# A graph network on one core: the preparation moved into the first gathers, and hop 0 with single outer products

## The chip, the cores and the metric

The kernel runs on one core of one Trainium2 chip. The metric is the device time of one execution in microseconds. Before the change three runs took 1715.54, 1716.27 and 1716.9 us; the median is 1716.27 us.

## The reference, cut to what matters

There are 50,000 nodes with 64 features and 25,000 edges (src, dst), sorted by dst. Layer 0 sums the normalised rows of the sources over each destination and puts every node through a small two-layer network. Layer 1 is an attention over three hops, with 8 heads of 8 features. What the change touches is the preparation of the degrees and hop 0:

```python
deg = segment_sum(ones, col, n);  deg_inv = where(deg > 0, deg ** -0.5, 0)
norm = deg_inv[row] * deg_inv[col] * edge_weight
Kj = relu(K[row] + ef)
M = segment_sum(norm * einsum('ehi,ehj->ehij', Kj, V[row]), col, n)   # hop 0
K = segment_sum(norm * Kj, col, n)
# hops 1 and 2:  M = segment_sum(norm * M[row], col, n)
```

## The kernel before, in words

The edges lie in 196 tiles of 128, and four tiles (EH) make a unit, so that each sweep has 49 units. Each engine runs one loop over a common tick `g`. All stages hang on that tick, and the order of the work on an engine is the order in which its loop body is written; semaphores tie the engines together. There is no planner.

- Ticks 0 to 48: the source rows of the edges are gathered by GpSimd (L541), normalised and kept in SBUF. Beside it VectorE and ScalarE do one unit of dense nodes every two ticks, and ScalarE counts the slot of each source (the `Sign` calls at L688).
- Ticks 49 to about 108: the destination rows are gathered, summed over equal destinations by TensorE and put through the network. The new row of each edge goes to `node_rows` in HBM.
- Ticks 109 (C0) to 159: hop 0. GpSimd gathers `node_rows` by source (L555). TensorE turns the rows (L947, L950), and makes keys, values and queries (L931 to L939). ScalarE copies keys (L718) and scaled values (L721) from PSUM banks 6 and 7 (`pkz`) to a ring of three SBUF tiles (`kvz`). VectorE makes the outer products of keys and values into PSUM banks 0 to 3, two tiles at once (`outer`, L1146), and adds each to the running sum (`join`, L1154). SyncE stores 1 MB of state (L501) and 256 KB of keys and values (L497) a unit. The function called at `NORMS_AT` makes the edge norms of two units in three small operations (L1300, L1307, L1313).
- Then hop 1 (D0), hop 2 (E0) and the output: gather the state, scale it, multiply by the queries. In hop 1 VectorE alternates L1354 (add) and L1356 (multiply).

The preparation of degrees is on VectorE in tick 55 (`PREP`): `prep_slots` (L1035 to L1062) passes the work to and fro between VectorE and TensorE three times (L918 to L924). In tick 56 ScalarE takes a root (L699) and `prep_rows` a reciprocal. In ticks 58 to 85 SyncE writes degrees and destinations into `node_rows`, 28 DMAs of 7 KB in pieces of 8 bytes (L457). `prep_out` is in tick 105, `prep_tiles` in tick 9. TensorE's preparation used bank 6, which also holds the segment ends until tick 53.

Of the kernel before, what the change touches and what calls it, by code (L numbers as in the profile page):

```python
# [14 lines left out]
P = 128  # L15
N = 50000
E = 25000
D = 64
# [51 lines left out]
PREP = B0 + 6  # L70
TAIL_AT = {PREP + 3 + i: i * TAIL for i in range(T // TAIL)}
# [113 lines left out]
def gnn(nc, x, edge_w, edge_attr, src_tm, dst_tm, dst_tmf, dst_row, ends, ends_col, masks, dst_pm, src_pm, src_row,  # L185
# [4 lines left out]
    d_tab, d_x1, d_kv = dram("node_rows", (ROWS, TW)), dram("x1_rows", (ROWS, D)), dram("kv_rows", (P, CU * 2 * W))  # L190
# [9 lines left out]
    with ExitStack() as ctx:  # L200
# [57 lines left out]
        kvz = ring("kv", [P, 2, EH, D], 3, s_front)  # L258
# [37 lines left out]
        kvf, thf, xf, hTf = (ring("kv_back", [P, 2, EH, D], RB, s_out), ring("row_back", [P, EH, D], RB, s_out),  # L296
# [22 lines left out]
        pprep = bank[6]  # L319
# [61 lines left out]
        def _(sync):  # L381
# [27 lines left out]
            def load_back(u):  # L409

                c = slice(u * EH, (u + 1) * EH)
                wait(sync, scaled_f, u - RB + 1)
                wait(sync, chained, EH * (u - RB + 1) + 1)
                sync.dma_start(gg[u % RB][:, 1, :, :], by_slot(d_g[1])[:, c, :]).then_inc(back_in[u % RB], 16)
                wait(sync, g0_set, u - RB + 1)
                sync.dma_start(kvf[u % RB][:, :, :, :].rearrange("p c k f -> p (c k f)"), d_kv[:, u * 2 * W:(u + 1) * 2 * W]).then_inc(back_in[u % RB], 16)
# [28 lines left out]
            for g in range(END + 1):  # L445
# [49 lines left out]
                if 0 <= u < CU:  # L495
                    sync.wait_ge(v_done, u + 1)
                    sync.dma_start(d_kv[:, u * 2 * W:(u + 1) * 2 * W], kvz[u % 3][:, :, :, :].rearrange("p c k f -> p (c k f)")).then_inc(kv_kept[u % 3], 16)  # L497
# [110 lines left out]
        def _(act):  # L608
# [13 lines left out]
            for g in range(END + 1):  # L622
# [74 lines left out]
                if g == PREP + 1:  # L697
                    act.wait_ge(prep_v, 3)
                    act.activation(tmp2[:, :], tmp[:, :], ACT.Sqrt).then_inc(prep_a, 1)  # L699
# [12 lines left out]
                if 0 <= u < CU:  # L712
                    p = pkz[u % 2]
                    act.wait_ge(kv_z, u + 1)
                    wait(act, outered, EH * (u - 2))
                    wait(act, kv_kept[u % 3], landed(u - 3, u % 3, 3))
                    parts = p[:, :].rearrange("p (k c f) -> p k c f", c=2, f=D)
                    act.activation(kvz[u % 3][:, 0, :, :], parts[:, :, 0, :], ACT.Relu).then_inc(k_done, 1)  # L718
                    act.wait_ge(wn_set, NORMED[u])
                    for k in range(EH):  # L720
                        ins = act.activation(kvz[u % 3][:, 1, k, :], parts[:, k, 1, :], ACT.Copy,  # L721
                                             scale=wn0[:, u * EH + k:u * EH + k + 1])
                    ins.then_inc(v_done, 1)
# [71 lines left out]
        def _(ten):  # L795
# [20 lines left out]
            for g in range(END + 1):  # L816
# [87 lines left out]
                if m is not None:  # L904
                    ten.wait_ge(h1_d, m + 1)
                    if m == LATE:
                        ten.wait_ge(prep_v, 3)
                    wait(ten, copied2_d, m)
                    turn_dense(turn2_bank(m), h1d[m % 2], turned2_d)
# [5 lines left out]

                if g == PREP:
                    ten.wait_ge(fixes_out, 1)
                    ten.matmul(pprep[:, 0:P], dpm[:, 0:1].to_broadcast([P, P]), ident[:, :], start=True, stop=True)  # L918
                    ten.matmul(pprep[:, 3 * P:3 * P + 1], shift[:, :], dpm[:, 0:1], start=True, stop=True).then_inc(prep_pe, 1)
                    ten.wait_ge(prep_v, 1)  # L920
                    ten.transpose(pprep[:, P:2 * P], carry[:, :], ident[:, :])
                    ten.matmul(pprep[:, 3 * P + 1:3 * P + 2], carry[:, :], tmp[:, T - 1:T], start=True, stop=True).then_inc(prep_pe, 1)
                    ten.wait_ge(prep_v, 2)
# [3 lines left out]
                if 0 <= u < CU:  # L927
                    p = pkz[u % 2]
                    wait(ten, v_done, u - 1)
# [95 lines left out]
        def _(vec):  # L1025
# [7 lines left out]
            def prep_slots():  # L1033
# [18 lines left out]
                vec.tensor_tensor(tail[:, :, 0], tmp[:, :], islast[:, :], ALU.mult).then_inc(prep_v, 1)  # L1052
                vec.wait_ge(prep_v, 1)
# [3 lines left out]
                vec.tensor_copy(carryT[:, :], pprep[:, P:2 * P]).then_inc(prep_v, 1)  # L1057
                vec.wait_ge(prep_v, 2)
# [80 lines left out]
            def outer(u, k):  # L1139

                shape = [P, 2 * HEADS, HD, HD]
                keys = flat(kvz[u % 3][:, 0, k:k + 2, :]).rearrange("p (c i) -> p c i", i=HD).unsqueeze(3).to_broadcast(shape)
                values = flat(kvz[u % 3][:, 1, k:k + 2, :]).rearrange("p (c j) -> p c j", j=HD).unsqueeze(2).to_broadcast(shape)
# [17 lines left out]
            for g in range(END + 1):  # L1161
# [98 lines left out]
                if g == 9:  # L1260
                    prep_tiles()
                if g == PREP:
                    prep_slots()
                if g == PREP + 1:
                    prep_rows()
                if g == C0 - 4:
                    prep_out()
# [113 lines left out]
                if 0 <= u < CU:  # L1381
                    vec.wait_ge(back_in[u % RB], back_rows(u))
                    o = slice(u * EH, (u + 1) * EH)
                    own.add(vec.tensor_tensor(kq[:, :, :], kvf[u % RB][:, 0, :, :], Q[:, o, :], ALU.mult))
# [15 lines left out]
                if 0 <= u < CU:  # L1400
# [3 lines left out]
                                      kvf[u % RB][:, 1, :, :].rearrange("p t (h j) -> p t h j", j=HD),  # L1404
# [116 lines left out]
```

## Time and profile before

| what | us |
|---|---|
| median of three runs | 1716.27 |
| the profiled execution | 1718.93 |
| its span | 1716.3 |
| VectorE busy | 1447.0 (84%) |
| TensorE busy | 1305.7 (76%) |
| GpSimd busy | 1208.4 (70%) |
| ScalarE busy | 990.9 (58%) |

The profiled execution is 2.7 us over the median. An engine's share is a mean over stages that have different limits, so each stage has to be read by itself: the window table gives busy time for a stretch, and the timeline gives start and length of each instruction with the idle time before it.

### The profile page before, as it was taken

How to read it: one execution, taken by the hardware profiler on the slowest of the kernel's cores; microseconds unless marked ns; L12 is line 12 of the kernel's file. 1: busy time of each engine (PE TensorE's matmuls, PEld its weight loads, DVE VectorE, ACT ScalarE, POOL GpSimd, SP SyncE). 2: the span in 40 equal slices, each digit the busy share in tenths (PEclk: the TensorE clock that was granted, in tenths of full speed). 3: DMA queues.
4: the chain of work that ended last, by engine and by line, in shares of the span. 5: the costliest groups of instructions: out<-in, count | busy, mean ns of one | idle time of the engine just before them, and what ended most of it. 6: DMA issues, size and time to landing. Idle time of an engine off the chain costs nothing. (4 is left out here: it accounts for less than half of the span.)

```text
span 1716.3 us, 21669 instructions
## 1 busy us (share of the span) xinstructions
PE 1305.7 (76%) x5794; PEld 800.1 (47%) x5794; DVE 1447.0 (84%) x2713; ACT 990.9 (58%) x2643; POOL 1208.4 (70%) x1185
## 2 busy tenths in 40 slices
PE   3889888899888757877863777775787999777771
PEld 3666666666666534544541233332233444455541
DVE  5888888799999849999997999995557788799991
ACT  4998987599999724444442555553555566233330
POOL 7777777577774077777736777774777777777776
PEclk8999998899999868878785889898798999888886
DMA  5444444477775459999985888885344544466640
GB/s 131 112 123 124 125 124 108 109 164 160 161 171 144 106 149 304 305 296 304 292 285 175 287 309 306 303 299 204 94 143 143 154 140 145 138 176 172 179 134 16
DMA packets 281215, 313.80 MB, mean 183 GB/s; under 512 B 169009, under 2 KB 198569, under 8 KB 268550
## 3 DMA queue, kind: packets, MB, share of 16 engines
q1 hardware_dynamic: 224166, 246.39, 46.6%
q0 software_dynamic: 56928, 66.04, 15.0%
q8 instruction: 47, 0.77, 0.2%
q14 instruction: 74, 0.61, 0.1%
HBM read 214.54 MB, written 161.32 MB: 219 GB/s over the span
## 5 line engine op out<-in xcount | busy, mean ns | idle before, releaser
L973 PE MATMUL bank<-product,ident 128*128 128x512 f32 (+1 forms) x800 | 385.0, 639 | 136.7 <-DVE product L1356 136.7
L579 POOL DMA_INDIRECT state<-state_hop,slot_of_src x392 | 396.4, 1011 | 125.8 <-issue 107.8
L748 ACT ACTIVATE bank<-state,norm 128x512 f32<-128x512 f32 x392 | 251.1, 679 | 255.4 <-DMA state<-state_hop,slot_of_src 218.9
L1356 DVE TENSOR_TENSOR product<-bank,queries 128x512 f32<-128x512 f32 x392 | 261.0, 687 | 91.3 <-ACT bank L748 89.8
L973 PEld LDWEIGHTS bank<-product,ident 128*128 128x128 f32 x800 | 162.1, 207 | 357.1 <-issue 186.2
L555 POOL DMA_INDIRECT row_of_src<-node_rows,pos_int x196 | 214.5, 1094 | 118.6 <-DMA node_rows<-row_new 59.1
L541 POOL DMA_INDIRECT x_edges<-in_x,dst_tiles x196 | 198.0, 1010 | 84.5 <-issue 48.0
L541 POOL DMA_INDIRECT x_edges<-in_x,src_tiles x196 | 198.5, 1013 | 62.6 <-issue 59.4
L595 POOL DMA_INDIRECT out<-rows,dst_out x196 | 194.7, 993 | 59.8 <-issue 58.2
L1354 DVE SCALAR_TENSOR_TENSOR acc<-acc,same_as_before,bank 128x512 f32<-128x512 f32 x196 | 144.9, 740 | 15.7 <-ACT bank L748 15.0
L1154 DVE SCALAR_TENSOR_TENSOR acc<-acc,same_as_before,bank 128x512 f32<-128x512 f32 x196 | 146.5, 747 | 12.3
L1015 PE MATMUL bank<-gg_squares,ident 128*128 128x256 f32 x294 | 100.1, 490 | 55.8 <-DVE gg_squares L1430 55.8
L1146 DVE TENSOR_TENSOR bank<-kv 128x1024 f32<-128x1024 f32 x98 | 120.3, 1227 | 5.1 <-ACT kv L721 4.7
L808 PE MATMUL bank<-bias_three,ones_three 3*128 3x512 bf16 (+1 forms) x246 | 83.7, 340 | 38.2 <-DVE x_edges L1254 23.6
L873 PE MATMUL bank<-dst_steps,from_here 128*128 128x197 f32 x392 | 85.0, 364 | 22.3 <-DVE end_flags L1123 17.1
L1015 PEld LDWEIGHTS bank<-gg_squares,ident 128*128 128x128 f32 x294 | 66.2, 240 | 74.9 <-DVE gg_squares L1430 65.1
L718 ACT ACTIVATE kv<-bank 128x256 f32<-128x256 f32 x49 | 18.8, 384 | 124.6 <-PE bank L936 118.4
L808 PEld LDWEIGHTS bank<-bias_three,ones_three 3*128 3x128 bf16 x246 | 22.6, 92 | 130.4 <-issue 126.0
L1420 DVE SCALAR_TENSOR_TENSOR gg<-gg,same_as_before 128x192 f32<-128x192 f32 x196 | 81.2, 414 | 2.0
L774 ACT ACTIVATE gg_squares<-gg 128x768 f32<-128x768 f32 x49 | 41.2, 840 | 68.1 <-DVE gg L1420 68.1
L873 PEld LDWEIGHTS bank<-dst_steps,from_here 128*128 128x128 f32 x392 | 69.2, 203 | 24.0 <-issue 21.8
L688 ACT ACTIVATE bank<-bank,src_slots 128x196 f32<-128x196 f32 x196 | 75.8, 387 | 4.9 <-PE bank L873 4.6
(219 smaller groups left out, 2844.4 us busy)
## 6 DMA issues: line engine op xcount, KB each, us to landing
state_hop<-acc SPq DMA_DIRECT2D x98, 1024.0 KB, 4.6
x_nodes<-in_x SPq DMA_DIRECT2D x49, 256.0 KB, 4.1
src_row<-in_src_row SPq DMA_DIRECT2D x49, 256.0 KB, 3.6
out<-out_rows SPq DMA_DIRECT2D x49, 256.0 KB, 4.2
dst_row<-in_dst_row SPq DMA_DIRECT2D x49, 256.0 KB, 3.6
kv_rows<-kv SPq DMA_DIRECT2D x49, 256.0 KB, 3.3
gg<-head_sums SPq DMA_DIRECT2D x98, 128.0 KB, 2.9
kv_back<-kv_rows SPq DMA_DIRECT2D x49, 256.0 KB, 2.9
```

Of the source, the lines that this page charges most:

```text
L541: pool.indirect_dma_start(out=xe[b][:, 0, k, :], out_offset=None, in_=x, in_offset=bass.IndirectOffsetOnAxis(ap=index[:, t:t + 1], axis=0) ...
L555: pool.indirect_dma_start(out=tg[u % RT][:, k, :], out_offset=None, in_=d_tab[0:SLOTS, :], in_offset=bass.IndirectOffsetOnAxis(ap=posi[:, ...
L579: pool.indirect_dma_start(out=mg[u % 4][:, k, :], out_offset=None, in_=d_m[hop - 1], in_offset=bass.IndirectOffsetOnAxis(ap=sidx[:, t:t + ...
L595: pool.indirect_dma_start(out=out, out_offset=bass.IndirectOffsetOnAxis(ap=dst_out[:, t:t + 1], axis=0), in_=rowf[u % NR][:, k, :], in_off ...
L748: act.activation(pw[t % len(pw)][:, :], mg[u % 4][:, k, :], ACT.Copy, scale=wn12[:, t:t + 1]).then_inc(weighted, 1)
L873: ins = ten.matmul(pair[:, 256 * k:256 * k + T + 1], gsel[u % 2][:, k * P:(k + 1) * P], delta[:, :], start=True, stop=True, skip_group_che ...
L973: ins = ten.matmul(ph[:, 0:k * D].rearrange("p (c j) -> p c j", j=HD), ident[:, :], part, start=(r == 0), stop=(r == HD - 1))
L1015: ins = ten.matmul(p[:, 0:W], ident[:, :], sqf[u % 3][:, :, :].rearrange("p (k c) j -> p k (c j)", k=HOPS)[:, k, :], start=False, stop=(k ...
L1146: vec.tensor_tensor(to, keys, values, ALU.mult).then_inc(outered, 2)
L1154: vec.scalar_tensor_tensor(accz[u % 3][:, k, :], before, same[:, t:t + 1], prz[k][:, :], ALU.mult, ALU.add).then_inc(acc_z, 1)
L1354: vec.scalar_tensor_tensor(acch[u % 3][:, k, :], before, same[:, t:t + 1], pw[t % len(pw)][:, :], ALU.mult, ALU.add).then_inc(acc_h, 1)
L1356: vec.tensor_tensor(ihj(pr[m % 2][:, u % 2 * EH + k, :]), ihj(pw[t % len(pw)][:, :]), over_j(Q[:, t, :]), ALU.mult).then_inc(multiplied, 1)
```

## The change

The preparation is cut up: `prep_slots` becomes three functions, called at VectorE's ticks 4, 6 and 8; `prep_rows` goes to tick 10, `prep_out` to 24, `prep_tiles` from 9 to 30. TensorE's part goes to ticks 3, 5 and 7 and to bank 7, ScalarE's root to tick 9, and the 28 DMAs of L457 to ticks 12 to 39. In hop 0 one outer product covers one tile, reads its values from PSUM (where ScalarE now scales them in place) and its keys from SBUF. Outer products and accumulations alternate, and the last accumulation of a unit follows the first outer product of the next. TensorE may overwrite the bank of keys and values of unit u-2 only when the outer products of u-2 are done. ScalarE copies the scaled values to SBUF in one further operation, for the store. The stored keys and values have another order in HBM, with pieces of the same size.

```diff
-PREP = B0 + 6
-TAIL_AT = {PREP + 3 + i: i * TAIL for i in range(T // TAIL)}
+TAIL_AT = {12 + i: i * TAIL for i in range(T // TAIL)}
...
-        kvz = ring("kv", [P, 2, EH, D], 3, s_front)
+        kvz = ring("kv", [P, EH, 2 * D], 3, s_front)
...
-        pprep = bank[6]
+        pprep = bank[7]
...
-                if g == PREP + 1:
+                if g == 9:
                     act.wait_ge(prep_v, 3)
                     act.activation(tmp2[:, :], tmp[:, :], ACT.Sqrt).then_inc(prep_a, 1)
...
-                    act.activation(kvz[u % 3][:, 0, :, :], parts[:, :, 0, :], ACT.Relu).then_inc(k_done, 1)
+                    act.activation(kvz[u % 3][:, :, 0:D], parts[:, :, 0, :], ACT.Relu).then_inc(k_done, 1)
                     act.wait_ge(wn_set, NORMED[u])
                     for k in range(EH):
-                        ins = act.activation(kvz[u % 3][:, 1, k, :], parts[:, k, 1, :], ACT.Copy,
+                        ins = act.activation(parts[:, k, 1, :], parts[:, k, 1, :], ACT.Copy,
                                              scale=wn0[:, u * EH + k:u * EH + k + 1])
-                    ins.then_inc(v_done, 1)
+                    own.add(ins)
+                    own.sync()
+                    act.activation(kvz[u % 3][:, :, D:2 * D], parts[:, :, 1, :], ACT.Copy).then_inc(v_done, 1)
...
+                    if m == 0:
+                        ten.wait_ge(prep_v, 3)
                     if m == LATE:
-                        ten.wait_ge(prep_v, 3)
+                        ten.wait_ge(fixes_out, 1)
...
-                    wait(ten, v_done, u - 1)
+                    wait(ten, outered, EH * (u - 1))
...
             def outer(u, k):
-                shape = [P, 2 * HEADS, HD, HD]
-                keys = flat(kvz[u % 3][:, 0, k:k + 2, :])...to_broadcast(shape)
-                values = flat(kvz[u % 3][:, 1, k:k + 2, :])...to_broadcast(shape)
-                to = quad[:, MW * k:MW * (k + 2)].rearrange("p (c i j) -> p c i j", i=HD, j=HD)
-                wait(vec, acc_z, EH * (u - 1) + k + 2)
-                vec.tensor_tensor(to, keys, values, ALU.mult).then_inc(outered, 2)
+                vs = pkz[u % 2][:, (2 * k + 1) * D:(2 * k + 2) * D]
+                wait(vec, acc_z, EH * (u - 1) + k + 1)
+                vec.tensor_tensor(ihj(prz[k][:, :]), over_j(kvz[u % 3][:, k, 0:D]), over_i(vs), ALU.mult).then_inc(outered, 1)
...
                     outer(u, 0)
+                if 0 < u < CU:
+                    join(u - 1, 3)
...
                 if 0 <= u < CU:
+                    outer(u, 1)
                     wait(vec, m0_kept[u % 3], landed(u - 3, u % 3, 3))
                     join(u, 0)
...
                 if 0 <= u < CU:
+                    outer(u, 2)
                     join(u, 1)
-                    outer(u, 2)
+                    outer(u, 3)
                     join(u, 2)
+                if u == CU - 1:
                     join(u, 3)
```

## Rows read from the trace of the kernel before

**Rows 1.** Windows of 50 us: busy us (count) by engine, then clock, DMA share, GB/s.
```profile
core 0: us, PE busy (x) PEld busy (x) DVE busy (x) ACT busy (x) POOL busy (x), PEclk, DMA share, GB/s
150.00:200.00 50.00, 44.01 (x298) 33.68 (x297) 42.84 (x78) 46.41 (x163) 38.42 (x39) 1.00 0.45 122
...
450.00:500.00 50.00, 44.31 (x287) 30.12 (x287) 49.55 (x114) 46.90 (x125) 35.15 (x36) 1.00 0.76 170
...
700.00:750.00 50.00, 38.88 (x194) 24.83 (x196) 47.70 (x66) 23.85 (x94) 39.31 (x36) 0.83 0.96 304
...
800.00:850.00 50.00, 40.58 (x190) 25.61 (x189) 46.31 (x68) 22.37 (x86) 39.34 (x36) 0.76 0.92 297
```

**Rows 2.** Waits of 120 to 180 us: total us, times, longest.
```profile
DVE stats L1184 <- ACT stats L695: 8.7, 6, 2.6
```

**Rows 3.** VectorE's timeline, ticks 5 and 6: start, length, instruction, idle before it.
```profile
38.82 1.22 DVE L1227 TENSOR_REDUCE stats<-x_nodes 128x16 f32<-128x1024 f32 x1 [1.84 <-ACT x_nodes L703]
...
44.22 0.30 DVE L1184 RECIPROCAL stats<-stats 128x24 f32<-128x24 f32 x1 [1.97 <-ACT stats L695]
```

**Rows 4.** VectorE's timeline, ticks 55 and 56.
```profile
311.24 0.16 DVE L1036 COPY next_first<-bank 128x1 f32<-128x1 f32 x1 [4.82 <-PE bank L919]
...
318.06 0.30 DVE L1184 RECIPROCAL stats<-stats 128x24 f32<-128x24 f32 x1
...
323.27 1.37 DVE L1067 RECIPROCAL dinv_slots<-prep_tmp 128x196 f32<-128x196 f32 x1
...
325.02 1.21 DVE L1224 TENSOR_REDUCE stats<-x_nodes 128x16 f32<-128x1024 f32 x1
```

**Rows 5.** ScalarE's timeline: the root that VectorE needs, ticks 55 and 105.
```profile
309.80 0.31 ACT L695 ACTIVATE stats<-stats,eps_col 128x24 f32<-128x24 f32 x1
...
589.69 0.32 ACT L695 ACTIVATE stats<-stats,eps_col 128x32 f32<-128x32 f32 x1 [0.63 <-DVE stats L1241]
```

**Rows 6.** VectorE's timeline, tick 105: first of prep_out, first after it.
```profile
589.56 0.35 DVE L1073 TENSOR_REDUCE prep_cols<-in_first 128x1 f32<-128x196 f32 x1
...
593.62 0.35 DVE L1184 RECIPROCAL stats<-stats 128x32 f32<-128x32 f32 x1
```

**Rows 7.** VectorE's timeline in hop 0: unit 1, one pair of units, the end.
```profile
629.87 1.29 DVE L1146 TENSOR_TENSOR bank<-kv 128x1024 f32<-128x1024 f32 x1 [0.41 <-issue]
...
742.22 0.16 DVE L1300 TENSOR_TENSOR dinv_of_src<-row_of_src,src_slots 128x8 f32<-128x8 f32 x1
...
746.43 1.53 DVE L1154 SCALAR_TENSOR_TENSOR acc<-acc,same_as_before,bank 128x512 f32<-128x512 f32 x2
...
753.47 0.16 DVE L1300 TENSOR_TENSOR dinv_of_src<-row_of_src,src_slots 128x8 f32<-128x8 f32 x1
...
903.04 0.26 DVE L1322 TENSOR_SCALAR prep_tmp<-dinv_of_src 128x196 f32<-128x196 f32 x1
```

**Rows 8.** VectorE's timeline in hop 1, alternating order, two steps apart.
```profile
948.30 0.75 DVE L1354 SCALAR_TENSOR_TENSOR acc<-acc,same_as_before,bank 128x512 f32<-128x512 f32 x1
...
950.82 0.74 DVE L1354 SCALAR_TENSOR_TENSOR acc<-acc,same_as_before,bank 128x512 f32<-128x512 f32 x1
```

**Rows 9.** The page's groups: busy us, mean ns of one, idle before, releaser.
```profile
L579 POOL DMA_INDIRECT state<-state_hop,slot_of_src x392 | 396.4, 1011 | 125.8 <-issue 107.8
...
L555 POOL DMA_INDIRECT row_of_src<-node_rows,pos_int x196 | 214.5, 1094 | 118.6 <-DMA node_rows<-row_new 59.1
...
L718 ACT ACTIVATE kv<-bank 128x256 f32<-128x256 f32 x49 | 18.8, 384 | 124.6 <-PE bank L936 118.4
```

**Rows 10.** TensorE's timeline in hop 0: the first matmul of four units.
```profile
747.01 0.37 PE L931 MATMUL bank<-bias_three,ones_three 3*128 3x512 bf16 x1 [0.89 <-ACT rows_turned L733]
...
751.57 0.37 PE L931 MATMUL bank<-bias_three,ones_three 3*128 3x512 bf16 x1 [0.88 <-ACT rows_turned L733]
...
816.08 0.58 PE L931 MATMUL bank<-bias_three,ones_three 3*128 3x512 bf16 x1 [1.60 <-ACT rows_turned L733]
...
823.44 0.58 PE L931 MATMUL bank<-bias_three,ones_three 3*128 3x512 bf16 x1 [0.78 <-ACT rows_turned L733]
```

**Rows 11.** Waits of 630 to 900 us: total us, times, longest.
```profile
ACT kv L721 <- DVE norm L1313: 20.7, 12, 6.1
```

More of the change, by code:

```diff
@@ L188, in dram @@
         return nc.dram_tensor(name, shape, F32, kind="Internal").ap()
-    d_tab, d_x1, d_kv = dram("node_rows", (ROWS, TW)), dram("x1_rows", (ROWS, D)), dram("kv_rows", (P, CU * 2 * W))
+    d_tab, d_x1, d_kv = dram("node_rows", (ROWS, TW)), dram("x1_rows", (ROWS, D)), dram("kv_rows", (SLOTS, 2 * D))
     d_m = [dram("state_hop0", (SLOTS, MW)), dram("state_hop1", (SLOTS, MW))]
@@ L295, in gnn @@
         qf = ring("norms", [P, 4, NH], 3, s_out)
-        kvf, thf, xf, hTf = (ring("kv_back", [P, 2, EH, D], RB, s_out), ring("row_back", [P, EH, D], RB, s_out),
+        kvf, thf, xf, hTf = (ring("kv_back", [P, EH, 2 * D], RB, s_out), ring("row_back", [P, EH, D], RB, s_out),
                              ring("x1_back", [P, EH, D], RB, s_out), ring("back_turned", [P, W], 3, s_out))
@@ L415, in load_back @@
                 wait(sync, g0_set, u - RB + 1)
-                sync.dma_start(kvf[u % RB][:, :, :, :].rearrange("p c k f -> p (c k f)"), d_kv[:, u * 2 * W:(u + 1) * 2 * W]).then_inc(back_in[u % RB], 16)
+                sync.dma_start(kvf[u % RB][:, :, :], by_slot(d_kv)[:, c, :]).then_inc(back_in[u % RB], 16)
                 wait(sync, turned_f, u - RB + 1)
@@ L496, in _ @@
                     sync.wait_ge(v_done, u + 1)
-                    sync.dma_start(d_kv[:, u * 2 * W:(u + 1) * 2 * W], kvz[u % 3][:, :, :, :].rearrange("p c k f -> p (c k f)")).then_inc(kv_kept[u % 3], 16)
+                    sync.dma_start(by_slot(d_kv)[:, u * EH:(u + 1) * EH, :], kvz[u % 3][:, :, :]).then_inc(kv_kept[u % 3], 16)
                 u = g - C0 - 2
@@ L914, in _ @@
                     turn_dense(ptd, zd[m % 2], turned1_d)
-                if g == PREP:
-                    ten.wait_ge(fixes_out, 1)
+                if g == 3:
                     ten.matmul(pprep[:, 0:P], dpm[:, 0:1].to_broadcast([P, P]), ident[:, :], start=True, stop=True)
                     ten.matmul(pprep[:, 3 * P:3 * P + 1], shift[:, :], dpm[:, 0:1], start=True, stop=True).then_inc(prep_pe, 1)
+                if g == 5:
                     ten.wait_ge(prep_v, 1)
@@ L922, in _ @@
                     ten.matmul(pprep[:, 3 * P + 1:3 * P + 2], carry[:, :], tmp[:, T - 1:T], start=True, stop=True).then_inc(prep_pe, 1)
+                if g == 7:
                     ten.wait_ge(prep_v, 2)
@@ L1052, in prep_slots, with prep_ends @@
                 vec.tensor_tensor(tail[:, :, 0], tmp[:, :], islast[:, :], ALU.mult).then_inc(prep_v, 1)
+            def prep_ends():
                 vec.wait_ge(prep_v, 1)
@@ L1057, in prep_slots, with prep_degrees @@
                 vec.tensor_copy(carryT[:, :], pprep[:, P:2 * P]).then_inc(prep_v, 1)
+            def prep_degrees():
                 vec.wait_ge(prep_v, 2)
@@ L1139, in outer @@
             def outer(u, k):
-                shape = [P, 2 * HEADS, HD, HD]
-                keys = flat(kvz[u % 3][:, 0, k:k + 2, :]).rearrange("p (c i) -> p c i", i=HD).unsqueeze(3).to_broadcast(shape)
-                values = flat(kvz[u % 3][:, 1, k:k + 2, :]).rearrange("p (c j) -> p c j", j=HD).unsqueeze(2).to_broadcast(shape)
-                to = quad[:, MW * k:MW * (k + 2)].rearrange("p (c i j) -> p c i j", i=HD, j=HD)
-                wait(vec, acc_z, EH * (u - 1) + k + 2)
-                vec.tensor_tensor(to, keys, values, ALU.mult).then_inc(outered, 2)
+                vs = pkz[u % 2][:, (2 * k + 1) * D:(2 * k + 2) * D]
+                wait(vec, acc_z, EH * (u - 1) + k + 1)
+                vec.tensor_tensor(ihj(prz[k][:, :]), over_j(kvz[u % 3][:, k, 0:D]), over_i(vs), ALU.mult).then_inc(outered, 1)
             def join(u, k):
@@ L1259, in _ @@
                     prep_bias()
-                if g == 9:
-                    prep_tiles()
[L1262 to L1267, printed above, removed]
+                if g == 4:
+                    prep_slots()
+                if g == 6:
+                    prep_ends()
+                if g == 8:
+                    prep_degrees()
+                if g == 10:
+                    prep_rows()
+                if g == 24:
+                    prep_out()
+                if g == 30:
+                    prep_tiles()
                 if g == CU + 3:
@@ L1383, in _ @@
                     o = slice(u * EH, (u + 1) * EH)
-                    own.add(vec.tensor_tensor(kq[:, :, :], kvf[u % RB][:, 0, :, :], Q[:, o, :], ALU.mult))
+                    own.add(vec.tensor_tensor(kq[:, :, :], kvf[u % RB][:, :, 0:D], Q[:, o, :], ALU.mult))
                     n_kq = own.n
@@ L1403, in _ @@
                     vec.tensor_tensor(gg[u % RB][:, 0, :, :].rearrange("p t (h j) -> p t h j", j=HD),
-                                      kvf[u % RB][:, 1, :, :].rearrange("p t (h j) -> p t h j", j=HD),
+                                      kvf[u % RB][:, :, D:2 * D].rearrange("p t (h j) -> p t h j", j=HD),
                                       scf[:, :].rearrange("p (t h) -> p t h", h=HEADS).unsqueeze(3).to_broadcast(
```

## The prediction, made before the changed kernel was run

> **What bounds the kernel now.** I read the window table first, then the waits of the stretches that differ, then the timelines of the engines where the change works, and last the page's groups for prices.
>
> The table [rows 1] separates three regimes. In the first gathers (150 to 200 us) no engine is full: ScalarE has 46.4 of 50 us and VectorE 42.8. The waits [rows 2] show VectorE held up by ScalarE's root, 8.7 us in six times, 1.45 us each time, once in two ticks. So VectorE has about 1.4 us to spare in two ticks and the stage goes round in a VectorE-ScalarE loop. In the second gathers (450 to 500 us) VectorE is busy 49.55 of 50 us: whatever it does there is time. In hop 0 (700 to 750 us) VectorE has 47.7 of 50 us, the DMA engines a share of 0.96, and TensorE a clock of 0.83, which is a mix of its two levels, 2.4 and 1.2 GHz.
>
> **The preparation: what goes.** In tick 55 VectorE waits 4.82 us for TensorE and then goes to and fro with it until 318.06 [rows 4]. ScalarE's root for that tick was done at 309.80 + 0.31 = 310.11 [rows 5]; it is what is late next. So 318.06 - 310.11 = 7.9 us go, of which I take 7.5, since ScalarE has a remainder of its tick to finish. In tick 56 `prep_rows` stands from 323.27 to 325.02 on the full VectorE: 1.75 us. In tick 105 `prep_out` stands from 589.56 to 593.62, 4.06 us [rows 6], while the root it hides was done at 589.69 + 0.32 = 590.01 [rows 5]: 3.5 us go, in the drain that the gathers of hop 0 wait for. Sum 12.7 us.
>
> **The preparation: what comes.** The parts are called at the end of even ticks, ahead of the large reductions, so a part's length is paid less what VectorE would have waited for ScalarE.
> - Tick 4: `prep_slots` without its ends, some 3.9 us (L1036 at 311.24 [rows 4] to the first answer of TensorE). VectorE waits 1.84 and 1.97 us in the next tick and a half [rows 3]: 3.8 us of cover, 0.1 us left. TensorE's answer was given a tick earlier.
> - Ticks 6 and 8: about 1.0 us each, under 1.4 us of cover: 0.
> - Tick 10: `prep_rows`, 1.75 - 1.4 = 0.4 us. ScalarE's root in tick 9 is one 0.3 us operation on the engine with the least room: 0.3 us.
> - Tick 24: `prep_out`, 4.06 - 1.4 = 2.7 us.
> - Tick 30: `prep_tiles`, four operations, about 1.5 us: 0.1 us more; in tick 9 it was covered too.
> - The 28 small DMAs move from a stretch with a DMA share of 0.76 to one with 0.45 [rows 1]. They stand on SyncE behind loads that are two ticks ahead of their use: 0. If that cover failed, each load would come up to some tenths late, 28 times: 5 us at most.
>
> Sum 3.6 us; bounds 0 (all covered) and 12 (no cover). Loops like this one do not catch up later, so I keep it as permanent. Net of the preparation: -9 us, between -13 and -1.
>
> **Hop 0 on VectorE.** From unit 1 to the end is 903.04 - 629.87 = 273.2 us for 48 units, 5.69 a unit; a pair takes 753.47 - 742.22 = 11.25 us [rows 7]. Two accumulations in a row take 1.53 us [rows 7], the second waits for the first. The alternating order stands in hop 1: from one L1354 to the next but one is 2.52 us, so an accumulation and a product cost 1.26 us [rows 8], with nothing waited for. The product there has one operand in PSUM, as the new one, and writes to SBUF, where the new one writes to PSUM; no row has that form. Its cost a step lies between 1.26 us and the present mean of 11.25 / 8 = 1.41 us; I take 1.26, being the same engine and size. Four steps make 5.04, the norms (three small operations for two units, their waits now hidden under a neighbour) 0.15: 5.2 us a unit, where 5.62 stood.
>
> **Hop 0 elsewhere.** What is late next?
> - GpSimd. A gather takes 1.011 us in hop 1 and 1.094 us in hop 0 [rows 9]; with 0.3 us of issue (107.8 us over 392) that is 1.31 or 1.39 us, four to a unit: 5.2 or 5.6 us. GpSimd is as slow as VectorE now, not slower. If the longer ones are held up by the products with both operands in SBUF, they fall to 1.31; I take 5.25 us.
> - DMA. The share 0.96 of 5.65 us is 5.4 us of work a unit. A share near one also counts queueing, so the floor is between 5.0 (no limit) and 5.4.
> - The loop of TensorE and ScalarE. At the high clock a unit takes 751.57 - 747.01 = 4.56 us, at the low clock 823.44 - 816.08 = 7.36 us [rows 10]. ScalarE gets one more copy of 256 columns, 0.38 us [rows 9], and a wait for its own result, some 0.1 us: 5.0 and 7.8 us. Before, TensorE could be nearly two units ahead of VectorE; now it may start a unit only after the products of the last but one, so it has one VectorE unit, 5.2 + 0.7 us, for a chain that takes about 4 us at the high clock and 6 at the low. Units at the low clock were mostly hidden; now each costs 7.8 - 5.35 = 2.45 us.
>
> I take 5.35 us for a unit at the high clock, which is 257 us for 48. How many units are at the low clock decides the rest. Before, the clock was 0.83 over the five windows from 650 to 900 us (0.76 in the last of those shown [rows 1]): a third of the time, some 13 units. Those stretches began after TensorE had stood still for 1.6 us and more, as at 816.08 [rows 10]; with gaps of 0.9 us it stayed at the high level. The long gaps came where ScalarE ran into the norms, 20.7 us in 12 waits [rows 11]; with TensorE held nearer to VectorE they mostly go. The new regular gap is 0.9 + 0.45 = 1.35 us, between the two. I take 4 units: 9.8 us. Hop 0 then takes 267 us, -6.5 us. Its bounds: 48 x 5.22 = 250.6 us, -22.6; and 13 units at the low clock, 35 x 5.35 + 13 x 7.8 = 289, +15.5.
>
> **Two rules beside the rows.** The gathers of hop 0 are longer than those of hop 1, 1.094 against 1.011 us [rows 9]. The Trainium skill, GPSIMD Engine Reference, Specifications, says that GpSimd shares its SBUF interfaces with VectorE and meets contention when a VectorE instruction has two SBUF inputs, as the old product has and the new one has not; by it the gathers fall to the 1.31 us with issue, without it they stay at 1.39, which would be 5.6 us a unit and hop 0 unchanged.
> The accumulation behind another takes 1.53 us for two [rows 7], while a step of two different operations takes 1.26 us [rows 8]. The Trainium skill, VectorE: DVE Perf Modes, The DRAIN you can't avoid, says that the next operation starts only when the pipe is empty, wait or no wait; by it the new order saves nothing (the second rival). The two rows speak against it.
>
> **How the sum stands to the runs.** The sum is -9 - 6.5 = -15.5 us, made against the profiled span of 1716.3 us. What lies around the span (1718.93 - 1716.3) stays. Taken off the median of 1716.27 this gives 1700.8 us; I say 1701.
>
> **Rivals.**
> 1. *TensorE's clock takes over hop 0.* The new wait leaves TensorE idle in every unit, the clock stays as it was or worse, and 13 units cost 2.45 us each that nothing hides: 1716.3 - 9 + 15.5 = 1723 us. It decides from about 10 units on (10 x 2.45 = 24.5, against 16 from the faster unit and 9 from the preparation). For it: the clock falls after a gap of 1.60 us. Against it: no drop after the gaps of 0.9, and 1.35 is nearer to those.
> 2. *The order saves nothing.* The operations stay at 1.41 a step, or GpSimd stays at 5.6 us a unit: only the preparation is won, 1707 us. For it: the form with values and result in PSUM has no row. Against it: hop 1's step.
> 3. *All of it is had.* TensorE stays at the high clock, DMA is no limit, and GpSimd's 5.22 us is the bound: 1716.3 - 9 - 22.6 = 1685 us. Against it: a DMA share of 0.96 already.
> 4. *The first gathers have no cover.* What is won later is lost at ticks 4 to 30: 12.7 - 12, with hop 0's -6.5: 1709 us. Against it: the 1.45 us waits.
>
> **How the numbers follow.** Forecast (1692 to 1706) 0.42; rival 1 0.26, of which a third lands within 0.2% and the rest beyond; rival 2 0.10; rival 3 0.15; rival 4 0.07. A measurement of this kernel tells 0.2%, 3.4 us, from no change. Faster 0.72, same 0.09, slower 0.19. The range takes in rival 3's value and most of rival 1's: 1685 to 1722.
>
> **What would show it.** Right: no idle VectorE of 4.8 us and no L1036 near 311 us; the stretch from unit 1 to L1322's successor 260 to 270 us; an accumulation and a product in 1.26 us; gathers in hop 0 near 1.01 us; the second gathers starting some 3 to 4 us later. Wrong: VectorE waiting for ScalarE's copy of the values in most units while TensorE's clock is under 0.8 (rival 1), steps of 1.4 us (rival 2), or second gathers 10 us later (rival 4).

## The result, and the profile of the changed kernel

The changed kernel takes 1692.9 us (median of 3 runs, 1691.5 to 1694.1) against 1716.27 us: a ratio of 0.9864, 95% interval 0.9841 to 0.9886. That is 23.4 us less, where the prediction had 1701 us, 15.5 us less. Its profiled execution has a span of 1691.1 us, 25.2 less than before.

The same windows as [rows 1], of the changed kernel:
```profile
core 0: us, PE busy (x) PEld busy (x) DVE busy (x) ACT busy (x) POOL busy (x), PEclk, DMA share, GB/s
150.00:200.00 50.00, 43.20 (x276) 33.57 (x277) 44.94 (x83) 44.30 (x151) 38.72 (x38) 0.94 0.54 123
450.00:500.00 50.00, 45.21 (x299) 31.49 (x295) 49.52 (x110) 47.51 (x126) 35.82 (x36) 1.00 0.63 159
700.00:750.00 50.00, 38.98 (x213) 24.93 (x213) 48.88 (x90) 27.70 (x108) 38.40 (x39) 0.91 0.98 325
800.00:850.00 50.00, 38.85 (x203) 24.91 (x204) 48.53 (x91) 26.42 (x100) 36.89 (x37) 0.89 0.98 319
```
In hop 0 VectorE is nearer to full (48.9 where it had 47.7), TensorE's clock is 0.91 and 0.89 where it was 0.83 and 0.76, and more bytes move.

The start of tick 55's second half and the end of hop 0 in VectorE's timeline:
```profile
313.11 0.30 DVE L1191 RECIPROCAL stats<-stats 128x24 f32<-128x24 f32 x1 [3.56 <-ACT stats L694]
...
615.31 0.18 DVE L1311 TENSOR_TENSOR dinv_of_src<-row_of_src,src_slots 128x8 f32<-128x8 f32 x1 [3.59 <-DMA row_of_src<-node_rows,pos_int]
615.81 0.70 DVE L1153 TENSOR_TENSOR bank<-kv,bank 128x512 f32<-128x512 f32 x1 [0.32 <-ACT kv L717]
...
880.14 0.26 DVE L1338 TENSOR_SCALAR prep_tmp<-dinv_of_src 128x196 f32<-128x196 f32 x1
```
In tick 55 the exchange with TensorE [rows 4] is gone; VectorE waits for ScalarE's root instead, which was named as next, and goes on 4.95 us earlier than in [rows 4] (313.11 against 318.06). From unit 1's first product to the end of hop 0 there are now 880.14 - 615.81 = 264.3 us; [rows 7] had 273.2.

The groups of the page that answer to [rows 9] and to the loop (busy us, mean ns of one, idle before, releaser):
```profile
L554 POOL DMA_INDIRECT row_of_src<-node_rows,pos_int x196 | 195.3, 997 | 114.9 <-issue 57.0
...
L1153 DVE TENSOR_TENSOR bank<-kv,bank 128x512 f32<-128x512 f32 x196 | 135.1, 690 | 14.8 <-issue 12.3
```
A gather of hop 0 went from 1094 to 997 ns, 19 us over 196 of them. The product has a new item: 14.8 us of idle VectorE ahead of it. The page calls most of it "issue", which is no releaser; ScalarE's and VectorE's timelines side by side give one:
```profile
702.70 0.38 ACT L724 ACTIVATE kv<-bank 128x256 f32<-128x256 f32 x1
```
```profile
703.17 0.69 DVE L1153 TENSOR_TENSOR bank<-kv,bank 128x512 f32<-128x512 f32 x1 [0.94 <-issue]
```
From unit 2 on, each of the 13 waits of 0.30 us and more ahead of the product ends 0.09 us after ScalarE's copy L724. The product itself doesn't read what L724 writes: its values stay in PSUM, where L720 has scaled them. But VectorE waits for `v_done`, which is raised only with the copy. Raising it with L720 is an obvious further variant that no run tried.

Where the 25.2 us come from, by the starts of single instructions in both traces:

| from, to | before | after | difference |
|---|---|---|---|
| start to the cast of pos_int (tick 52) | 288.4 | 291.4 | +3.0 |
| from there to the first gather of row_of_src | 314.8 | 301.8 | -13.0 |
| first gather to unit 1's first product | 26.7 | 22.6 | -4.1 |
| unit 1's first product to the end of hop 0 | 273.2 | 264.3 | -8.9 |
| the rest (hops 1 and 2, output) | 813.3 | 811.0 | -2.3 |

### The profile page after: what moved, and what is told of

Read it like the earlier page. It is cut to its first block and busy times, and to the rows that moved or that the text cites. A ratio compares the mean times of both kernels' runs of the same rounds, so it can differ in the third digit from the quotient of the medians.

```text
span 1691.1 us, 21721 instructions
## 1 busy us (share of the span) xinstructions
PE 1292.2 (76%) x5794; PEld 794.1 (47%) x5794; DVE 1438.1 (85%) x2811; ACT 1005.2 (59%) x2692; POOL 1187.2 (70%) x1185
## 3 DMA queue, kind: packets, MB, share of 16 engines
q0 software_dynamic: 56928, 66.04, 15.5%
## 5 line engine op out<-in xcount | busy, mean ns | idle before, releaser
L554 POOL DMA_INDIRECT row_of_src<-node_rows,pos_int x196 | 195.3, 997 | 114.9 <-issue 57.0
L540 POOL DMA_INDIRECT x_edges<-in_x,dst_tiles x196 | 197.5, 1008 | 77.4 <-issue 48.9
L1370 DVE SCALAR_TENSOR_TENSOR acc<-acc,same_as_before,bank 128x512 f32<-128x512 f32 x196 | 145.3, 741 | 15.4 <-ACT bank L749 14.8
L1153 DVE TENSOR_TENSOR bank<-kv,bank 128x512 f32<-128x512 f32 x196 | 135.1, 690 | 14.8 <-issue 12.3
L1019 PE MATMUL bank<-gg_squares,ident 128*128 128x256 f32 x294 | 95.1, 472 | 53.4 <-DVE gg_squares L1446 53.4
L809 PE MATMUL bank<-bias_three,ones_three 3*128 3x512 bf16 (+1 forms) x246 | 83.1, 338 | 36.8 <-DVE x_edges L1261 22.6
L1019 PEld LDWEIGHTS bank<-gg_squares,ident 128*128 128x128 f32 x294 | 62.0, 224 | 71.2 <-DVE gg_squares L1446 62.5
L809 PEld LDWEIGHTS bank<-bias_three,ones_three 3*128 3x128 bf16 x246 | 22.6, 92 | 129.2 <-issue 125.1
```

What stands on the lines that cost most here:

```text
L540: pool.indirect_dma_start(out=xe[b][:, 0, k, :], out_offset=None, in_=x, in_offset=bass.IndirectOffsetOnAxis(ap=index[:, t:t + 1], axis=0) ...
L554: pool.indirect_dma_start(out=tg[u % RT][:, k, :], out_offset=None, in_=d_tab[0:SLOTS, :], in_offset=bass.IndirectOffsetOnAxis(ap=posi[:, ...
L1019: ins = ten.matmul(p[:, 0:W], ident[:, :], sqf[u % 3][:, :, :].rearrange("p (k c) j -> p k (c j)", k=HOPS)[:, k, :], start=False, stop=(k ...
L1153: vec.tensor_tensor(ihj(prz[k][:, :]), over_j(kvz[u % 3][:, k, 0:D]), over_i(vs), ALU.mult).then_inc(outered, 1)
L1370: vec.scalar_tensor_tensor(acch[u % 3][:, k, :], before, same[:, t:t + 1], pw[t % len(pw)][:, :], ALU.mult, ALU.add).then_inc(acc_h, 1)
```

## The experiments

Two things stayed open: where hop 0's 13.0 us (4.1 + 8.9) come from, twice what was forecast, and what bounds hop 0 now. My theory after the two traces: the preparation gives 10 us; in hop 0 the shorter gathers and the shorter steps of VectorE give the rest, and part of that is lost again in waits of VectorE for the loop over TensorE and ScalarE. Rivals: the preparation helps hop 0 too; the order alone counts; DMA, at a share of 0.98, is the limit. Before the change GpSimd and VectorE ran hop 0 at nearly the same pace, 5.59 us a unit (272.7 us for 195 steps of a gather) and 5.62, so both had to get faster. No run with times near 1700 us leaves one of the two as it was and changes only the other.

One thing is needed to read the numbers. The first runs of experiments 1, 3 and 4 and that of experiment 2 were made on one chip, the second runs of 1 and 4 and those of 5 and 6 on another, and the second run of 3 and those of 7 on a third. On the first and the third every kernel that ran there, the one before among them, took 2045 to 2111 us, with the same durations of VectorE's, ScalarE's and GpSimd's single instructions but with idle stretches on the engines, and with a granted clock of 0.78 to 0.82 over the whole run, where the others have 0.88 to 0.92. ScalarE's timeline in the changed kernel on one of them:
```profile
776.66 0.60 ACT L734 ACTIVATE rows_turned<-bank 128x512 f32<-128x512 f32 x1 [10.78 <-remote]
787.97 0.38 ACT L717 ACTIVATE kv<-bank 128x256 f32<-128x256 f32 x1 [10.71 <-remote]
```
Twice in a row ScalarE stands still for over 10 us. "remote" means that a semaphore rose and the profile names no instruction for it. In the second case it is the semaphore of TensorE's keys and values: it rose at 787.94 us, 7.2 us after the recorded end of their last matmul (780.78; such ends are modelled). What delayed it the trace doesn't say. From these eight runs I read durations and distances of neighbouring instructions and give the ratios, but take no microseconds of the whole from them. The four runs of the second chip (below: the middle set) ran beside a before of 1714.13 us. The changed kernel itself wasn't run in that set, so comparisons with it go by the ratios to the before of each set.

**1. The moved preparation alone** (prep_only, prep_only_b): the changed kernel's preparation, hop 0 as before.
```
 if g == 4:  prep_slots()      if g == 10: prep_rows()
 if g == 6:  prep_ends()       if g == 24: prep_out()
 if g == 8:  prep_degrees()    if g == 30: prep_tiles()
 # outer, join, kv, the norms: as before
```


> Leaves hop 0 as it was before and takes only the moved preparation. Theory A (the two parts are worth what the milestones of the two traces say, 10 us for the preparation and 13 us for hop 0, and they add): 1706 us, 10 below before, with the first gather of row_of_src 10 us earlier. Rival B (part of the 13 us of hop 0 comes from the preparation, since hop 0 starts from an idle stretch that is 10 us shorter and keeps TensorE's clock): under 1703 us, and a hop 0 of less than 299 us from its first gather, against 299.8 before. Rival C (the preparation was hidden and only shifted a wait): above 1712 us.

> The same edit as prep_only (only the moved preparation, hop 0 as before), on another chip if there is one, since on the first all kernels took 2070 to 2100 us with idle stretches of 10 us and more on every engine. Theory A (10 us from the preparation, 13 from hop 0, they add): 1706 us, ratio 0.994. Rival B (part of hop 0's gain comes from the preparation): 1703 us or less and a hop 0 under 299 us from its first gather. Rival C (hidden): 1712 us or more.

The first run gave 2075.6 us, ratio 0.995 (0.990 to 1.000). The second gave 1707.1 us, ratio 0.995 (0.993 to 0.997), so 8.6 us less, between 5 and 12 (7.0 by the medians). Its first gather of row_of_src starts at 595.5 us, 7.7 earlier than before and not theory A's 10, and from unit 1's first product to the cast of slot_of_src it takes 274.3 us, before 274.1. By the measure that the expectation named, from the first gather to the end of hop 0, it is 299.2 us against 299.8. So the preparation gives 8 to 10 us and hop 0 nothing from it, or less than 1 us: theory A holds in the main, B and C fall.

**2. Hop 0 alone** (hop0_only): the preparation as before, hop 0 as changed.
```
-PREP = ...; prep in ticks 4 to 30
+PREP = B0 + 6; prep in ticks 9, 55, 56 and 105, as before
```


> Leaves the preparation as it was before and takes only hop 0's new order, products and norms. Theory A (parts add): 1703 us, hop 0 of 287 us from its first gather, ticks 55 and 56 unchanged. Rival B (hop 0's gain rests on the shorter idle stretch before it): 1708 us or more, hop 0 of 292 us or more. Under both the preparation's stalls at ticks 55, 56 and 105 stand as before.

2102.6 us, ratio 1.0065 (1.0025 to 1.0105), on the first chip. Neither theory had this: on that chip hop 0's change gains nothing or costs a little. Its gathers are 999 ns each there too, and VectorE's idle time before the product is 89 us. That a shorter step is no use where the engines stand still anyway is my reading, not tested. What the edit alone does on the chip of the middle set was not measured; I infer it from experiment 1 and the table above.

**3. Both operands in SBUF** (sbuf_values, sbuf_values_b).
```
-vs = pkz[u % 2][:, (2 * k + 1) * D:(2 * k + 2) * D]
+vs = kvz[u % 3][:, k, D:2 * D]
```


> As the changed kernel, but the outer product reads its scaled values from SBUF (kv) instead of PSUM; nothing else is moved. Theory A (GpSimd's gather issue is held while VectorE reads two operands from SBUF; the changed kernel gained in hop 0 because no product does so any more): the row_of_src gathers go from 1.00 us each back to a mean of 1.1 us or more, GpSimd's unit from 5.2 to 5.6 us or more, and the kernel takes 1700 to 1712 us. Rival B (the gathers were slow before for another reason, and the order of VectorE is what counts): gathers stay at 1.00 us and the time within 2 us of 1693.

> The same edit as sbuf_values. On the first chip, where VectorE stood idle a lot, the gathers of row_of_src took 1.024 us in the mean against 0.997, some up to 1.55; before, with double products that read two operands from SBUF, 1.094. Theory A (a gather that meets such a product is held): mean of 1.03 us or more, the gathers end 6 us or more later than 847 us, and the time is 1697 to 1705 us. Rival B (the hold comes only from the double products of 1024 elements): gathers at 1.00 us and the time within 3 us of the changed kernel.

2090.5 us (0.9991, 0.9958 to 1.0024) and 2074.2 us (0.9938, 0.9887 to 0.9990). The times say nothing on the question, the gathers do: 1024 and 1030 ns in the mean, under the 1.1 us that theory A of the first run wanted, at the 1.03 us of the second. GpSimd's timeline before, and with the values in SBUF:
```profile
741.83 1.00 POOL L555 DMA_INDIRECT row_of_src<-node_rows,pos_int  x1 [0.30 <-PE bank L950]
743.14 1.25 POOL L555 DMA_INDIRECT row_of_src<-node_rows,pos_int  x1 [0.30 <-issue]
744.69 1.00 POOL L555 DMA_INDIRECT row_of_src<-node_rows,pos_int  x1 [0.30 <-DVE norm L1313]
745.99 1.20 POOL L555 DMA_INDIRECT row_of_src<-node_rows,pos_int  x1 [0.30 <-issue]
```
```profile
814.79 1.49 POOL L554 DMA_INDIRECT row_of_src<-node_rows,pos_int  x1 [0.30 <-issue]
...
820.50 1.22 POOL L554 DMA_INDIRECT row_of_src<-node_rows,pos_int  x1 [0.30 <-issue]
```
Before, nearly every second gather is long. All long ones start inside a double product, and only 2 of the 109 others do. The gather at 743.14 starts within this one of VectorE's:
```profile
742.30 1.23 DVE L1146 TENSOR_TENSOR bank<-kv 128x1024 f32<-128x1024 f32 x1
```
and with the values in SBUF the one at 814.79 within this single product:
```profile
814.72 0.70 DVE L1153 TENSOR_TENSOR bank<-kv 128x512 f32<-128x512 f32 x1 [2.07 <-issue]
```
The sizes follow one pattern. A gather that starts x us into a double product takes about 1.00 + (1.09 - x) us: at 743.14, 0.84 us in, 1.25 us. This holds within 0.01 us for all 87, and for the 72 and 89 long ones of experiment 1. With single products 33 of 36 fit 0.56 in place of 1.09 (814.79: 0.07 us in, 1.49 us). It is as if the gather stood still until shortly before the product's recorded end and then took its usual 1.00 us.
Over hop 0 87 of 196 gathers were over 1.05 us, 18.6 us in excess, which is all of the gathers' gain: they took 272.7 us from the first to the last before and 253.8 after. The changed kernel has not one over 1.05 us, and neither has any of the eight other runs whose products read their values from PSUM. With the values in SBUF there are 16 and 20 again, up to 1.58 us, 5.4 and 5.9 us in excess. 33 of the 36 start inside a product, in its first 0.44 us, and the other three at most 0.03 us ahead of one. So the hold comes back with the operands (theory A in its mechanism), but for single products on a VectorE that often stands idle it is a third in size. What it would cost in time with a full VectorE is open.

**4. Pairs in place of alternation** (in_pairs, in_pairs_b).
```
-outer 0, join 3 of the unit before, outer 1, join 0, outer 2, join 1, outer 3, join 2
+outer 0, outer 1, join 0, join 1, outer 2, outer 3, join 2, join 3
```


> As the changed kernel, with single products and accumulations but in the order two products, two accumulations, two products, two accumulations, so that one accumulation follows directly on the one it needs. Theory A (the alternation saves the wait between dependent accumulations, 1.53 us for two against 1.26 us for product and accumulation together; VectorE comes first with 5.4 us a unit or more): 1698 to 1708 us. Rival B (VectorE has slack beside the gathers and DMA at 5.1 us a unit, the order saves nothing): within 2 us of 1693.

> The same edit as in_pairs. In the first trace two dependent accumulations took 1.44 us of pitch and two products 1.20, so VectorE's unit is 5.28 us against 5.04 in alternation, without norms. Theory A (VectorE's unit sets hop 0, 49 units): 0.24 us a unit, 12 us more, 1703 to 1706 us. Rival B (the gathers' 5.2 us or DMA set the pace just as well): 2 to 6 us more, 1695 to 1699 us. Rival C: no change.

First run 2093.4 us, ratio 1.0017 (0.9983 to 1.0052). Second run 1696.5 us, 0.9897 (0.9865 to 0.9929), against the changed kernel's 0.9864 (0.9841 to 0.9886): 5.7 us more at the central values, with intervals that overlap, so rival B's 2 to 6 us at best and not theory A's 12; rival C, no change, isn't excluded. The four executions lie at 1690.5, 1692.9, 1700.1 and 1700.5 us, and the profiled one is the shortest: in it unit 1 to the end of hop 0 takes 259.8 us, 4.5 less than in the changed kernel's trace. VectorE's timeline in it shows the step:
```profile
622.81 1.29 DVE L1153 TENSOR_TENSOR bank<-kv,bank 128x512 f32<-128x512 f32 x2
624.01 1.53 DVE L1161 SCALAR_TENSOR_TENSOR acc<-acc,same_as_before,bank 128x512 f32<-128x512 f32 x2
625.45 1.29 DVE L1153 TENSOR_TENSOR bank<-kv,bank 128x512 f32<-128x512 f32 x2
```
Two products have a pitch of 1.20 us, two dependent accumulations 1.44, a unit 5.28 us. In alternation it is 1.26 a step, 5.04 a unit; 0.24 us over 49 units is 12 us. With the norms counted, units without a wait take 5.36 us against 5.10 and 5.18 in turn, which is 10 us over 48. They were not lost, because VectorE's waits ahead of the product shrank with them, from 14.8 to 4.2 us. The slower VectorE hides the loop; the faster one runs into it. What the executions of 1700 us did is not known, they have no trace.

**5. The norm with the keys** (keys_scaled). It gives the reference's result as long as no edge weight is negative, which these are not (0 to 1).
```
-act.activation(kvz[..., 0:D], parts[:, :, 0, :], Relu)
-[wait for the norm] 4 x activation(parts V, parts V, Copy, scale=norm)   # in place, PSUM
-[wait for the own write] act.activation(kvz[..., D:2*D], parts V, Copy)
+act.activation(kvz[..., D:2*D], parts[:, :, 1, :], Copy)                 # raw values
+[wait for the norm] 4 x activation(kvz K, parts K, Relu, scale=norm)
```


> As the changed kernel, but the norm (never negative for these edge weights, 0 to 1) is applied with the relu of the keys instead of with the values: ScalarE copies the raw values to kv before it waits for the norm, then relus and scales the keys in four instructions; nothing is written in place, one copy of 0.39 us and one wait on its own write fall away, and VectorE reads the values raw from PSUM. Theory A (in part of the units, after low-clock stretches, the loop TensorE to ScalarE to VectorE comes last, 12.3 us of VectorE's waits): those waits shrink, 1684 to 1690 us. Rival B (VectorE and the gathers set hop 0 alone): within 2 us of 1693.

1680.9 us (1679.4 to 1683.0), ratio 0.9799 (0.9774 to 0.9823): better than both kernels, 11 us below the changed one by the ratios, and more than theory A had it (1684 to 1690). The first matmul of units in TensorE's timeline, changed kernel:
```profile
641.59 0.58 PE L935 MATMUL bank<-bias_three,ones_three 3*128 3x512 bf16 x1 [0.78 <-ACT rows_turned L734]
648.95 0.58 PE L935 MATMUL bank<-bias_three,ones_three 3*128 3x512 bf16 x1 [0.78 <-ACT rows_turned L734]
...
667.07 0.37 PE L935 MATMUL bank<-bias_three,ones_three 3*128 3x512 bf16 x1 [0.99 <-ACT rows_turned L734]
672.01 0.37 PE L935 MATMUL bank<-bias_three,ones_three 3*128 3x512 bf16 x1 [1.27 <-ACT rows_turned L734]
```
and norm with the keys:
```profile
719.75 0.37 PE L934 MATMUL bank<-bias_three,ones_three 3*128 3x512 bf16 x1 [0.89 <-ACT rows_turned L733]
724.31 0.37 PE L934 MATMUL bank<-bias_three,ones_three 3*128 3x512 bf16 x1 [0.89 <-ACT rows_turned L733]
```
At the high clock the loop falls from 4.94 to 4.56 us a unit, and TensorE gets ahead again after a unit at the low clock (7.36 us in both). VectorE's waits before its product in hop 0 are 3.8 us where they were 14.8, and unit 1 to the end of hop 0 takes 253.1 us where it took 264.3: the 11 us are these waits. The edit does two things at once, it drops one instruction and puts the copy ahead of the wait for the norm; which of them counts was not separated. Its windows, with those of the next experiment behind them:
```profile
700.00:750.00 50.00, 39.13 (x218) 25.03 (x216) 50.00 (x94) 25.66 (x100) 38.11 (x40) 0.93 1.00 335
800.00:850.00 50.00, 39.65 (x214) 25.06 (x213) 50.00 (x92) 24.99 (x99) 37.18 (x38) 0.90 1.00 330
```

**6. Fillers on TensorE** (warm2): two products of 256 columns a unit, on the bank that the unit overwrites next.
```
+for _ in range(2):
+    ten.matmul(p[:, 0:W], ident[:, :], Wkv, start=True, stop=True, ...)
 ten.wait_ge(copied_z, u + 1)
```


> As the changed kernel, with two filler products of 256 columns a unit on TensorE in hop 0, written to the PSUM bank that the unit's keys and values are about to overwrite; their result is not used. It asks what TensorE's clock costs in hop 0. Theory A (the low-clock units with a loop of 7.4 us against 5.0 cost hop 0 the 4 us of waits at VectorE that follow them, fillers keep the clock): granted clock in hop 0 over 0.95, 1686 to 1691 us. Rival B (fillers lengthen TensorE's own part by 0.85 us a unit and the loop gets later than VectorE): 1697 us or more. Rival C (no effect either way): within 2 us.

1680.2 us (1678.9 to 1682.1), ratio 0.9795 (0.9770 to 0.9819).
```profile
700.00:750.00 50.00, 45.99 (x256) 29.49 (x254) 50.00 (x94) 29.25 (x110) 38.21 (x39) 1.00 1.03 335
800.00:850.00 50.00, 44.88 (x243) 28.94 (x244) 49.05 (x91) 27.50 (x104) 37.95 (x39) 1.00 1.01 325
```
The clock is 1.00 where it was 0.91 and 0.89, VectorE is busy for 50.00 of 50 us, and its waits before the product are 2.0 us in all of hop 0. The gain is larger than theory A had it (some 12 us for 2 to 7), since all 14.8 us of waits go and not just a few. Work that nobody uses pays here because TensorE's part has room in the unit. Unit 1 to the end of hop 0 takes 250.9 us. And rival "DMA is the limit" falls: with VectorE full, its units at 5.10 and 5.18 us in turn, DMA follows, at a share of up to 1.03.

**7. The rest on the third chip** (after_b, keys_pairs, keys_warm). The first is the changed kernel; the second keys_scaled with the order of experiment 4; the third keys_scaled with the fillers of experiment 6.

> The changed kernel again, on the chip of the others of this set, so that they are compared with it in the same rounds: 1690 to 1693 us, with 10 to 16 us of VectorE's waits for ScalarE's values in hop 0.

> keys_scaled with the order of in_pairs (two products, two accumulations). In keys_scaled VectorE is busy for 50.00 of 50 us from 715 us on, so there the order must show. Theory A (alternation is worth 0.24 us a unit wherever VectorE comes last; in the changed kernel its worth went into waits for the loop over TensorE and ScalarE): 9 to 12 us over keys_scaled, 1689 to 1693 us. Rival B (the order is worth nothing even then, since the gathers take 5.2 us a unit): within 3 us of keys_scaled, 1681 to 1684 us.

> keys_scaled with the two fillers of warm2. Theory A (both take away the same wait, that of VectorE for the loop; what is left, gathers at 1.30 us each and VectorE at 5.1 us a unit, neither touches): 1677 to 1681 us, not 12 us less than either. Rival B (the two gains are of different kinds and add): 1667 to 1671 us.

2076.3 us (0.9992, 0.9953 to 1.0031), 2080.3 us (1.0017, 0.9972 to 1.0061) and 2065.1 us (0.9949, 0.9914 to 0.9983). All three expectations of time are missed by the chip. That the changed kernel gains nothing on it is a result of its own. VectorE's waits there, 750 to 1110 us, and in the first profile of the same kernel, 593 to 905 us:
```profile
DVE bank L1153 <- issue: 77.3, 34, 8.2
```
```profile
DVE bank L1153 <- issue: 12.3, 13, 2.2
```
34 waits of up to 8.2 us stand before the product, 77.3 us where the expectation had 10 to 16; that a faster VectorE only waits longer there is argued from them. Whether alternation is worth 12 us once the loop is out of the way (keys_pairs), and whether the gains of experiments 5 and 6 add (keys_warm), stays open; that each alone already leaves VectorE full speaks against adding, and so do the gathers: from first to last they take 253.6 to 253.8 us in the changed kernel and in experiments 4, 5 and 6 alike, and hop 0 with 253.1 and 250.9 us for 48 units is at their pace already.

## Why the prediction was right, step by step

- **Preparation, removed: 12.7.** Held. Tick 55: the new wait of VectorE ends 4.95 us earlier though everything runs 3.0 us later by then, so 7.95 went, for 7.5. Ticks 56 and 105 together with it: 13.0 us, by the table.
- **Preparation, added: 3.6.** Held, 3.0 in this trace; 5.2 in experiment 1's and 2.9 to 4.5 in the three others of the middle set. VectorE's timeline of tick 4 and 5 answers to [rows 3]:
```profile
40.04 0.36 DVE L1056 TENSOR_TENSOR row_tails<-prep_tmp,last_here 128x196 f32<-128x196 f32 x1
...
43.88 0.30 DVE L1191 RECIPROCAL stats<-stats 128x24 f32<-128x24 f32 x1 [0.18 <-ACT stats L694]
```
  The part from 36.55 us on ends at 40.4, and the next reciprocal starts at 43.88, no later than 44.22 in [rows 3]; of 1.97 us of wait 0.18 are left. The net of -9 was -10.0 in the traces here, -7.7 in the trace of experiment 1 and -8.6 by its ratio. The rival of no cover is out. VectorE's waits for the root (150 to 200 us, behind the moved parts) were 6.2 us and are 4.1.
- **VectorE's unit: 5.2.** Held: in the 264.3 us it is busy for 249.3, 5.19 us a unit. The step of 1.26 us that no row had for this form came out to the hundredth:
```profile
704.44 0.69 DVE L1153 TENSOR_TENSOR bank<-kv,bank 128x512 f32<-128x512 f32 x1
705.04 0.74 DVE L1161 SCALAR_TENSOR_TENSOR acc<-acc,same_as_before,bank 128x512 f32<-128x512 f32 x1
705.70 0.69 DVE L1153 TENSOR_TENSOR bank<-kv,bank 128x512 f32<-128x512 f32 x1
```
  A product begins 0.66 us after an accumulation that lasts 0.74, an accumulation 0.60 after a product of 0.69. Each starts 0.08 or 0.09 us ahead of the recorded end of the one before. The Trainium skill (VectorE: DVE Perf Modes, The DRAIN you can't avoid) says not only what the prediction took from it, but also that a next operation that is not held starts earlier, and that half is the one that this pair agrees with. The second rival is out in that form. In time, though, the order was worth some 6 us at most by the central values (experiment 4).
- **GpSimd: 5.25.** Held, 253.8 us for 49 units, 5.18. The rule on shared interfaces (the Trainium skill, GPSIMD Engine Reference, Specifications) agrees with the rows of experiment 3: in hop 0 no long gather without a product of two SBUF operands, and long ones again with it.
- **The unit I took, 5.35 us, and DMA's floor.** Too high: nothing but VectorE and its waits set the unit. 48 x 0.16 = 8 us too much.
- **Low clock: 9.8 us from 4 units.** Too low: VectorE is idle for 15.0 us in these 48 units, 12.3 of them ahead of the product, in 13 waits. Six of TensorE's units took 6.9 us and more, and eleven, part of them at the low clock, 5.9 to 6.5 us; of these I had counted none. The loop at the high clock was right (4.95 for 5.0 us), so was the regular gap (1.27 for 1.35); at the low clock a unit took 7.36 us, as before, and not 7.8. What failed is the reading of the gaps. The prediction took 1.35 us as nearer to the gaps that keep the clock, but ahead of ten of these eleven units TensorE had stood still for no more than 1.36 us.
- **Hop 0 in sum: 267 us for the 48 units.** 264.3. The two errors have opposite signs and nearly cancel, which is luck, and 2.4 us are left.
- **The beginning of hop 0: not in the sum.** This term is what was missing, 4.1 us. I had counted from unit 1's product on, so a shift ahead of it could not show. Before, unit 1's norm waits 6.76 us for its gathers, at 629.30; after, 3.59 us, at 615.31. The cause is open. In the trace before, the 1 MB store of unit 0's states is issued at 622.7, ahead of their landing; after, unit 0's last accumulation is put behind unit 1's first product, and the store goes out at 617.2, when they have landed. That the store is the cause is argued from this order and was not tried by itself. With hop 0 as before (experiment 1) the distance from the first gather to unit 1's product is 25.9 us. With pairs (experiment 4), where the store goes out early again, it is 24.4 us, and 22.5 and 23.9 us in experiments 5 and 6, where it goes out late. So at most a part of the 4.1 us follows the store.
- **The first rival** was the right mechanism in the wrong size: TensorE's clock costs hop 0 some 12 us (experiment 6), not the 32 us of 13 units at 2.45.
- **Two slips of the sum of chances.** Forecast and rivals 2, 3 and 4 make 0.74 for faster, where 0.72 stands, and rival 1's 1723 us lies just outside the range that is said to take in most of it.

Of the 7.5 us between 15.5 and the traces' 23.0, 4.1 are the beginning, 2.4 the 48 units, 1.0 the preparation. Another 2.3 us come from the stages after hop 0, 1.8 of them in the output stage; no run tells why.

## What to carry to other kernels

When a change makes the full engine faster, ask which loop it was hiding: here some 10 us of a shorter VectorE step, against the same kernel in pairs, went into waits for a TensorE-ScalarE loop that had got 0.4 us longer through the same change, and taking one copy out of that loop gave 11 us. Count a stage from its first transfer, not from its steady part, since its start moves too. And before keeping a gain of 1%, see it on more than one chip: on another one there was none.

## What the runs showed of the hardware

- A gather's issue on GpSimd, 1.00 us else, lasts mostly 1.15 to 1.25 us and up to 1.64 in the kernel before when it starts inside a VectorE product of 1024 elements with both operands in SBUF, longer by what is left of the product's first 1.09 us, and up to 1.58 us with products of 512 elements, there by what is left of 0.56 us; beside products with one operand in PSUM it stays at 0.99 to 1.01 us, 196 times of 196.
- A product and an accumulation of 0.69 and 0.74 us that don't need each other's result repeat every 1.26 us, each starting 0.08 or 0.09 us ahead of the recorded end of the one before. Two products and two accumulations, the second of which needs the first, take 2.64 us in place of 2.52.
- Fillers that made TensorE busy for 46.0 instead of 39.0 of 50 us raised its granted clock (700 to 750 us) from 0.91 to 1.00 and made the kernel some 12 us faster.
- At a DMA share of 0.98 (325 GB/s) the stage was still not bound by DMA: a shorter unit moved 335 GB/s, at shares of 1.00 and 1.03.
- Two chips ran every kernel tried on them, the one before too, at 2045 to 2111 us where the others took 1679 to 1720, with VectorE's and GpSimd's single instructions as long as elsewhere and engines idle for up to 10 us and more without an instruction named as releaser. What held them is open.
